# Cross attention on one core: the denominators' last sum moves from a transfer to TensorE, with another order of work in a step

## The chip, the cores and the metric

The kernel runs on one core of a Trainium2 chip. The metric is the device time of one execution in microseconds (us). The kernel before takes 3871.87 us (median of 3 runs, 3871.11 to 3872.05).

The engines are named as in the profile: PE is TensorE (PEld are its weight loads), DVE is VectorE, ACT is ScalarE, POOL is GpSimd, and SP issues transfers only.

## The reference, cut to what matters

```
q = (x @ Wq + bq)      # 4 batches x 1024 rows, 32 heads of 32
k = ctx @ Wk + bk      # 4 batches x 1601 rows,  8 key heads of 32
v = ctx @ Wv + bv
scores = einsum('bkgld,bksd->bkgls', q, k) / sqrt(32) + mask
attn   = softmax(scores, axis=-1)                 # over the 1601 keys
out    = einsum('bkgls,bksd->bkgld', attn, v) @ Wo + bo + x
result = layernorm(out) * gamma + beta
```

Each key head serves four query heads. All data is float32. The softmax's denominators, one sum over 1601 keys for each head and query row, are what the change is about.

## The kernel before, in words

There are three stages: `project` (q, k and v, stored to DRAM), `attend` (from about 0.8 to 3.48 ms of the span), and `output` (the last projection and the layer norm). Only `attend` is touched.

`attend` makes 64 steps: 8 blocks of 512 query rows times 8 key heads. A step takes 512 rows and the 4 query heads of one key head. Its 1601 keys are cut into 13 tiles of 128 (the last has 65). A step's work on TensorE is of five kinds, and the string `ORDER` writes it out as letters, 99 of them, in the order in which TensorE runs them:

- L (52 in a step: 13 tiles x 4 heads): one logit tile, keys x rows, into one of 3 PSUM banks `logit` (L866). ScalarE takes the exponential of it into the SBUF buffer `weights` (L1030). An L waits until the bank's previous user is read: the L three before it.
- S (32): half of a row of scores for the **next** step, two matmuls into one of 2 PSUM tiles `score` (L821). VectorE reduces it to a maximum (L972). An S waits for the reduction of the S two before it.
- M (13): one weights tile times its values, accumulated in `mixed` (L876, through `sum_heads`: four heads side by side, each on 32 columns of the array, in two passes: 8 matmul records). With `FIRST_MIX = 1` the first M of a step handles the last tile of the step before.
- T (1): the row maxima are transposed (L852); ScalarE and VectorE copy them (L1036, L984) and SP carries them to the next step's operands.
- P (1): the denominators of the step before, a matmul with ones (`denominators`, through `sum_heads`, L876); ScalarE copies them out (L1048). P shares the 3 `logit` banks with L and T.

The order is fixed by hand in `ORDER`; all engines but GpSimd loop over the same string. Each engine takes its instructions strictly in that order.

GpSimd sums the weights tiles of a step for the denominators. Tiles 0, 1, 3, 4, 6, 7, 9, 10 and 12 (the tuple `POOL`) are added by eight tensor_tensor instructions into `sum_pool` (`add`, L736). The other four, `REST = (2, 5, 8, 11)`, are summed by three accumulating transfers that GpSimd issues: tiles 5, 8 and 11 are added onto tile 2's own buffer, the base buffer (`add_rest`, L747). A fourth transfer, `merge` (L754), adds the base buffer to `sum_pool`; it is issued behind the first add of the next step, and waits for all eight adds and all three transfers. P waits for that transfer (`rest_merged`). The weights buffers are rings: 2 base buffers, 4 for the tiles of `POOL`, 2 for tiles 5, 8 and 11; ScalarE waits before it writes a buffer until the tile that was there is mixed and summed (in `exponents`). For the base buffer that wait is on `rest_merged`. The last step of all has its own end, `last_denominators`.

Of the kernel before, what the change touches and what calls it, by code (L numbers as in the profile page):

```python
# [22 lines left out]
ALU = mybir.AluOpType  # L23
ACT = mybir.ActivationFunctionType

P = 128
# [436 lines left out]
def attend(nc, mask_flat, q_dram, k_dram, v_dram, a_dram, d_dram, r_dram, wo_dram, ident, mask_size, qk_store, wo_spare, wo_in):  # L463
    QUAD = 4
# [3 lines left out]
    REST = (2, 5, 8, 11)  # L468
# [3 lines left out]
    LATE = 10  # L472
    NPOOL = len(POOL) - 1

    ORDER = "LLLSLSLLSLMSLLSLMMSLLSLLSLSLLSLMMSLLSLLSLSLLSLMMSLLSLLSLSLLSLPMMLSLSLLLSLSTMMLLSLLSLSLLSLSLLSLMMSLS"
    FIRST_MIX = 1
    LO_AT = 24
    assert [ORDER.count(k) for k in "LSMTP"] == [ST * G, 2 * NROW, ST, 1, 1]
    BANKS = 3
    USES = [k for k in ORDER if k in "LTP"]  # L480
    assert len(USES) % BANKS == 0
    TURN, SUMS = USES.index("T"), USES.index("P")
# [20 lines left out]
    def ring(st):  # L503

        return (POOL, RINGS[0], BASES) if st in POOL else (REST[1:], RINGS[1], BASES + RINGS[0])

    def buffer(s, st):

        if st == REST[0]:
            return s % BASES  # L510
        tiles, size, first = ring(st)
        return first + (s * len(tiles) + tiles.index(st)) % size
# [9 lines left out]
    with ExitStack() as held:  # L522
# [3 lines left out]
        def sem(name):  # L526
            return held.enter_context(nc.semaphore(name))
# [11 lines left out]
        weights = [sb(f"weights{i}", [P, G, LQ]) for i in range(BASES + sum(RINGS))]  # L539
        sum_pool = [sb(f"sum_pool{i}", [P, G, LQ]) for i in range(2)]  # L540
        ones = sb("ones", [P, HD])
# [6 lines left out]
        logit = [held.enter_context(nc.psum_tensor(f"logit{i}", [P, LQ], F32)) for i in range(BANKS)]  # L548
# [23 lines left out]
        pool_added = sem("pool_added")  # L572
        pool_seen = sem("pool_seen")
        rest_added = sem("rest_added")
        rest_merged = sem("rest_merged")
        mix_done = sem("mix_done")
        mixed_copied = sem("mixed_copied")
        denom_done = sem("denom_done")
# [138 lines left out]
        @block.gpsimd  # L717
        def _(pool):

            nc.gpsimd.memset(ones[:], 1.0).then_inc(const_done, 1)  # L720
            for i, k in enumerate(k_sb):
                pool.wait_ge(const_done, 1 + i)
                nc.gpsimd.memset(k[STACK:SHIFT, :].bitcast(F32), 1.0).then_inc(const_done, 1)

            def add(quad, s, n):

                step, st = quad * QUAD + s, POOL[n + 1]
                w = min(P, S - st * P)
                pool.wait_ge(exp_done, quad * (QUAD * ST * G) + (s * ST + st + 1) * G)
                if n == 0:  # L730
                    pool.wait_ge(denom_done, step + 1)
                    first = weights[buffer(s, POOL[0])]
                else:
                    pool.wait_ge(pool_added, step * NPOOL + n)
                    first = sum_pool[s % 2]
                nc.gpsimd.tensor_tensor(sum_pool[s % 2][0:w], first[0:w], weights[buffer(s, st)][0:w], ALU.add).then_inc(pool_added, 1)  # L736

            def add_rest(quad, s, k):

                step, st = quad * QUAD + s, REST[k]  # L740
                pool.wait_ge(exp_done, quad * (QUAD * ST * G) + (s * ST + st + 1) * G)
                if k == 1:
                    pool.wait_ge(mix_done, quad * (QUAD * ST) + (s * ST + REST[0] + 1 + MIX0))
                else:
                    pool.wait_ge(rest_added, step * (16 * (len(REST) - 1)) + 16 * (k - 1))
                pool.sem_inc(pool_seen, 1)
                pool.dma_start(weights[buffer(s, REST[0])][:], weights[buffer(s, st)][:], accum_op=ALU.add).then_inc(rest_added, 16)  # L747

            def merge(step, s):

                pool.wait_ge(pool_added, step * NPOOL + NPOOL)
                pool.wait_ge(rest_added, step * (16 * (len(REST) - 1)) + 16 * (len(REST) - 1))
                pool.sem_inc(pool_seen, 1)
                pool.dma_start(sum_pool[s % 2][:], weights[buffer(s % QUAD, REST[0])][:], accum_op=ALU.add).then_inc(rest_merged, 16)  # L754

            def sums(quad, s, first=False, last=False):
                for n in range(NPOOL):
                    if last and POOL[n + 1] >= LATE:
                        break
                    for k, st in enumerate(REST):  # L760
                        if k and POOL[n] < st < POOL[n + 1]:
                            add_rest(quad, s, k)
                    add(quad, s, n)
                    if n == 0 and not first:
                        merge(quad * QUAD + (s - 1), s - 1)

            pool.wait_ge(flag_done, 1)
            any_mask = pool.value_load(flag[0:1, 0:1], min_val=0, max_val=1)

            def clamp_max(a, lts):  # L770
                for lt in lts:
                    pool.wait_ge(mask_in[lt], a * 16 + 16)

                    pool.sem_inc(mask_max_seen, 1)
                    nc.gpsimd.tensor_scalar(mask_max[:, lt, :], mask_max[:, lt, :], -FAR, None, ALU.max).then_inc(mask_ready[lt], KVH // QUAD)

            def clamp_exp(a):
                pool.wait_ge(mask_exp_in, a * (16 * NLT) + 16 * NLT)

                pool.sem_inc(mask_exp_seen, 1)  # L780

                nc.gpsimd.tensor_scalar(mask_exp[:], mask_exp[:], -FAR, None, ALU.max).then_inc(mask_exp_ready, KVH // QUAD)

            def queries(a, first=False, final=False):
                with pool.If(any_mask > 0):
                    clamp_exp(a)
                for n in range(KVH):
                    if n >= KVH - 2 and not final:
                        with pool.If(any_mask > 0):
                            clamp_max(a + 1, range(0, 2) if n == KVH - 2 else range(2, NLT))  # L790
                    sums(a * (KVH // QUAD) + n // QUAD, n % QUAD, first and n == 0, final and n == KVH - 1)

            with pool.If(any_mask > 0):
                clamp_max(0, range(NLT))
            queries(0, first=True)
            for a in range(1, NLQ - 1):
                queries(a)
            queries(NLQ - 1, final=True)

        @block.tensor  # L800
        def _(pe):
# [71 lines left out]
            def sum_heads(out, lhs, rhs, w, start, stop):  # L873

                for h in range(G):
                    last = nc.tensor.matmul(out[h * HD:(h + 1) * HD, :], lhs, rhs[0:w, h, :], start=start, stop=stop)  # L876
                return last
# [11 lines left out]

            def denominators(step, s):  # L890

                pe.wait_ge(rest_merged, step * 16 + 16)
                sum_heads(logit[SUMS % BANKS], ones[:], sum_pool[s % 2], P, True, True).then_inc(denom_done, 1)

            def last_denominators():

# [10 lines left out]
            def quad_steps(quad, masked, first=False, last=False):  # L907
                for s in range(QUAD):
                    u = k = 0
                    tile = s * ST - FIRST_MIX  # L910
                    for work in ORDER:
                        if work == "L":
# [96 lines left out]
        def _(act):  # L1009
# [3 lines left out]
            def exponents(quad, s, u):  # L1013
                n = USES[:u].count("L")
                st, h = n // G, n % G
                before, old = tile_before(s, st)
                if h == 0 and not (isinstance(quad, int) and quad == 0 and before < 0):

                    if st == REST[0]:
                        act.wait_ge(rest_merged, quad * (16 * QUAD) + (16 * before + 16))  # L1020
                    else:
                        act.wait_ge(mix_done, quad * (QUAD * ST) + (before * ST + old + 1 + MIX0))

                        if old in POOL:
                            act.wait_ge(pool_added, quad * (QUAD * NPOOL) + (before * NPOOL + max(POOL.index(old), 1)))
                        else:
                            act.wait_ge(rest_added, quad * (QUAD * 16 * (len(REST) - 1)) + 16 * (before * (len(REST) - 1) + REST.index(old)))
                act.wait_ge(logit_done, quad * (QUAD * ST * G) + ((s * ST + st) * G + h + 1 + LOGITS0))
                w = min(P, S - st * P)
                nc.scalar.activation(weights[buffer(s, st)][0:w, h, :], logit[u % BANKS][0:w, :], ACT.Exp).then_inc(exp_done, 1)  # L1030
# [19 lines left out]
            def quad_steps(quad, first=False, last=False):  # L1050
                for s in range(QUAD):
                    u = mixes = 0
                    for work in ORDER:
                        if work == "L":
# [259 lines left out]
```

## Time and profile before

| | us |
|---|---|
| time, median of 3 runs | 3871.87 |
| the profiled execution's own time | 3873.77 |
| its span | 3872.1 |
| PE busy in the span | 3769.2 |
| DVE busy | 2496.9 |
| ACT busy | 2033.2 |
| POOL busy | 2895.5 |

The page gives the busy time of each engine, its groups of instructions by line, and the issues of transfers. "Busy" of PE includes the modelled end of each matmul, so a PE that is busy all the time is not at its peak. The timeline merges instructions of one kind that follow one another: a row has its start, the time that it covers, and behind x the number of instructions. In the timeline the weight loads (PEld) show best when TensorE begins a piece of work. POOL's L747 and L754 rows are issues of transfers; the transfers themselves run on the DMA queues.

### The profile page before, as it was taken

The numbers are of one execution on the slowest core, as the hardware profiler recorded it, in microseconds if no ns is written. First come the engines' busy times: TensorE is split into PE (matmuls) and PEld (weight loads), VectorE is DVE, ScalarE is ACT, GpSimd is POOL, SyncE is SP. The second block draws the span as 40 slices with busy tenths as digits, with TensorE's granted clock in tenths as the row PEclk, the third lists the DMA queues.
The fourth block names the chain that finished last, engine by engine and source line by source line (L and its number), as shares of the span: only waits on it lengthen the run. The fifth ranks groups of instructions, "written<-read, shape, count | busy, mean of one in ns | idle before, by whom it ended". The sixth has DMA issues, their size and how long they took to land. (4 is left out here: it accounts for less than half of the span.)

```text
span 3872.1 us, 55400 instructions
## 1 busy us (share of the span) xinstructions
PE 3769.2 (97%) x20306; PEld 2379.7 (61%) x20306; DVE 2496.9 (64%) x2904; ACT 2033.2 (53%) x3854; POOL 2895.5 (75%) x1104
## 2 busy tenths in 40 slices
PE   8999999789999999999999999999999999988998
PEld 7998888545555555555555555555555555536886
DVE  3334444477777777777777777777777777725665
ACT  2222112126666666666666666676666666661110
POOL 1111111139999999999999999999999999984555
PEclk9999999869999999999999999999999999998999
DMA  5344555647667667667667667677677677667664
GB/s 176 136 150 177 201 198 200 246 85 152 146 146 155 145 145 158 143 145 159 146 144 158 145 146 158 141 151 155 139 155 151 141 155 149 146 150 220 194 191 125
DMA packets 294100, 611.94 MB, mean 158 GB/s; under 512 B 131696, under 2 KB 168688, under 8 KB 261360
## 3 DMA queue, kind: packets, MB, share of 16 engines
q0 software_dynamic: 58080, 337.15, 38.7%
q1 hardware_dynamic: 232528, 265.54, 25.7%
q10 hardware_dynamic: 3264, 6.29, 0.5%
q8 instruction: 134, 2.20, 0.2%
q14 instruction: 94, 0.77, 0.1%
HBM read 244.50 MB, written 96.99 MB: 88 GB/s over the span
## 5 line engine op out<-in xcount | busy, mean ns | idle before, releaser
L972 DVE TENSOR_REDUCE half_max<-score 128x1 f32<-128x800 f32 (+1 forms) x2048 | 1893.7, 986 | 714.2 <-PE score L821 710.2
L1030 ACT ACTIVATE weights<-logit 128x512 f32<-128x512 f32 (+1 forms) x3328 | 1732.4, 602 | 791.6 <-PE logit L866 765.6
L736 POOL TENSOR_TENSOR sum_pool<-sum_pool,weights 128x2048 f32<-128x2048 f32 x446 | 2125.6, 4766 | 29.6 <-ACT weights L1030 2.5
L821 PE MATMUL score<-qk_store 96*128 96x400 f32 (+1 forms) x4096 | 1212.2, 378 | 14.9 <-DMA qk_store<-k_parts 10.4
L866 PE MATMUL logit<-qk_store 98*128 98x512 f32 (+1 forms) x3328 | 1199.5, 417 | 2.3 <-ACT weights L1030 2.2
L821 PEld LDWEIGHTS score<-qk_store 96*128 96x128 f32 x4096 | 688.5, 191 | 552.6 <-DVE half_max L972 397.5
L876 PE MATMUL mixed<-weights,v_sb 128*32 128x512 f32 x6656 | 807.8, 599 | 0.7 <-ACT weights L1030 0.7
L866 PEld LDWEIGHTS logit<-qk_store 98*128 98x128 f32 (+1 forms) x3328 | 607.8, 185 | 264.0 <-ACT weights L1030 135.1
L876 PEld LDWEIGHTS mixed<-weights,v_sb 128*32 128x32 f32 x6656 | 177.0, 109 | 393.2 <-ACT weights L1030 218.6
L736 POOL TENSOR_TENSOR sum_pool<-weights 128x2048 f32<-128x2048 f32 x64 | 313.7, 4901 | 63.6 <-ACT weights L1030 63.6
L450 POOL DMA_DIRECT2D q_parts<-o_hi x64 | 34.5, 540 | 306.1 <-DVE o_lo L412 149.3
L1192 PE MATMUL acc<-qk_store,a_hi 128*128 128x512 f32 x576 | 187.0, 397 | 25.1 <-DVE a_lo L1227 25.1
L347 ACT ACTIVATE o_hi<-summed,bq_scaled 128x512 fp32r<-128x512 f32 x64 | 44.1, 689 | 304.0 <-PE summed L259 274.3
L325 ACT CAST t_hi<-turned 128x512 fp32r<-128x512 f32 x168 | 95.6, 585 | 141.8 <-PE turned L254 141.8
L407 DVE TENSOR_SCALAR full<-summed,bq_scaled 128x512 f32<-128x512 f32 x64 | 48.0, 751 | 188.5 <-ACT o_hi L347 188.5
L747 POOL DMA_DIRECT2D weights<-weights x191 | 165.9, 868 | 0.0
L1281 POOL TENSOR_TENSOR total<-total,beta_row 128x1024 f32<-128x1024 f32 x32 | 100.4, 3139 | 76.3 <-DVE total L1248 76.3
L1274 POOL TENSOR_TENSOR total<-total,bo_row 128x1024 f32<-128x1024 f32 x32 | 89.6, 2806 | 85.4 <-DMA total<-in_x 85.2
L456 POOL DMA_DIRECT2D v_rows<-v_store x52 | 28.1, 540 | 160.1 <-DMA v_rows<-v_store 101.5
L1192 PEld LDWEIGHTS acc<-qk_store,a_hi 128*128 128x128 f32 x576 | 109.4, 190 | 52.6 <-issue 26.0
L372 DVE TENSOR_TENSOR t_lo<-turned,t_hi 128x512 fp32r<-128x512 f32 x168 | 113.1, 685 | 42.6 <-ACT t_hi L325 42.4
L259 PE MATMUL summed<-t_hi,wq_hi 128*128 128x512 f32 x512 | 134.6, 404 | 0.0
(87 smaller groups left out, 2772.4 us busy)
## 6 DMA issues: line engine op xcount, KB each, us to landing
weights<-weights POOLq DMA_DIRECT2D x191, 1024.0 KB, 7.3
sum_pool<-weights POOLq DMA_DIRECT2D x63, 1024.0 KB, 7.0
qk_store<-q_parts SPq DMA_DIRECT2D x192, 256.0 KB, 3.9
qk_store<-k_parts SPq DMA_DIRECT2D x192, 200.1 KB, 5.4
rows<-in_ctx SPq DMA_DIRECT2D x26, 1024.0 KB, 5.1
landing<-in_mask_Bx1xSxS_ff SPq DMA_DIRECT2D x32, 800.5 KB, 5.5
rows<-in_x SPq DMA_DIRECT2D x16, 1024.0 KB, 5.1
q_parts<-o_hi POOLq DMA_DIRECT2D x64, 256.0 KB, 2.4
```

The source lines that it names most:

```text
L259: last = nc.tensor.matmul(acc, lhs, rhs, start=(n == 0), stop=(n == len(pairs) - 1))
L325: nc.scalar.copy(t_hi[par][:, t, :], turned[t % 2][:]).then_inc(hi_done, 1)
L372: nc.vector.tensor_tensor(t_lo[par][:, t, :], turned[t % 2][:], t_hi[par][:, t, :].bitcast(F32), ALU.subtract).then_inc(lo_done, 1)
L736: nc.gpsimd.tensor_tensor(sum_pool[s % 2][0:w], first[0:w], weights[buffer(s, st)][0:w], ALU.add).then_inc(pool_added, 1)
L747: pool.dma_start(weights[buffer(s, REST[0])][:], weights[buffer(s, st)][:], accum_op=ALU.add).then_inc(rest_added, 16)
L821: last = nc.tensor.matmul(score[j][:, c, 0:w], q_sb[buf][0:STACK, h, lt * P:(lt + 1) * P], k_sb[buf][0:STACK, start:start + w], start=True ...
L866: last = nc.tensor.matmul(bank[0:w, :], k_sb[s][:, keys], q_sb[s][:, h, :], start=True, stop=not masked, skip_group_check=masked)
L876: last = nc.tensor.matmul(out[h * HD:(h + 1) * HD, :], lhs, rhs[0:w, h, :], start=start, stop=stop)
L972: nc.vector.tensor_reduce(half_max[m // NROW % 2][:, k % G, k // G, j:j + 1], score[j][:, :, 0:HALVES[j][2]], mybir.AxisListType.XY, ALU.m ...
L1030: nc.scalar.activation(weights[buffer(s, st)][0:w, h, :], logit[u % BANKS][0:w, :], ACT.Exp).then_inc(exp_done, 1)
L1192: last = nc.tensor.matmul(acc[j * NT + t][:, n, :], a[:, k, cols], w[k][:, out_cols], start=(k == 0 and m == 0), stop=(k == KVH - 1 and m ...
L1281: nc.gpsimd.tensor_tensor(total[r][:], total[r][:], beta_row[:], ALU.add).then_inc(final, 1)
```

## The change

`merge`, its call and its semaphore go. `denominators` takes two sums into one bank: first the base buffer, as soon as the step's three transfers are in, then `sum_pool`, when the eight adds are done. ScalarE's wait for the base buffer is now on the denominators of two steps back. `ORDER` is another string of the same letters.

```
-    ORDER = "LLLSLSLLSLMSLLSLMMSLLSLLSLSLLSLMMSLLSLLSLSLLSLMMSLLSLLSLSLLSLPMMLSLSLLLSLSTMMLLSLLSLSLLSLSLLSLMMSLS"
+    ORDER = "LLSSMSLLSLLSLLSLLSLSLLSLLSLLSLLSLLSLLSMMMMPSLLSLLSLLSLSLLSLLSLLSMMMSLLSLTSMMSLSLLLSLSLLSLLSLLSLMMML"
@@ GpSimd
-            def merge(step, s):
-                pool.wait_ge(pool_added, step * NPOOL + NPOOL)
-                pool.wait_ge(rest_added, step * (16 * (len(REST) - 1)) + 16 * (len(REST) - 1))
-                pool.sem_inc(pool_seen, 1)
-                pool.dma_start(sum_pool[s % 2][:], weights[buffer(s % QUAD, REST[0])][:], accum_op=ALU.add).then_inc(rest_merged, 16)
...
-                    if n == 0 and not first:
-                        merge(quad * QUAD + (s - 1), s - 1)
@@ TensorE, denominators
-                pe.wait_ge(rest_merged, step * 16 + 16)
-                sum_heads(logit[SUMS % BANKS], ones[:], sum_pool[s % 2], P, True, True).then_inc(denom_done, 1)
+                pe.wait_ge(rest_added, step * (16 * (len(REST) - 1)) + 16 * (len(REST) - 1))
+                sum_heads(logit[SUMS % BANKS], ones[:], weights[buffer(s % QUAD, REST[0])], P, True, False)
+                pe.wait_ge(pool_added, step * NPOOL + NPOOL)
+                sum_heads(logit[SUMS % BANKS], ones[:], sum_pool[s % 2], P, False, True).then_inc(denom_done, 1)
@@ ScalarE, exponents
                     if st == REST[0]:
-                        act.wait_ge(rest_merged, quad * (16 * QUAD) + (16 * before + 16))
+                        act.wait_ge(denom_done, quad * QUAD + (before + 3))
```

## Rows read from the trace of the kernel before

**Rows 1.** The page, busy us and share of each engine.
```profile
PE 3769.2 (97%) x20306; PEld 2379.7 (61%) x20306; DVE 2496.9 (64%) x2904; ACT 2033.2 (53%) x3854; POOL 2895.5 (75%) x1104
```
**Rows 2.** The windows view, full steps 0 to 62: busy us, granted clock, DMA share.
```profile
841.10:3441.00 2599.90, 2596.91 (x14408) 1425.95 (x14407) 1876.05 (x2142) 1788.87 (x3470) 2525.37 (x755) 1.00 0.70 148
```
**Rows 3.** The waits view, 1000 to 3400 us: us in total, times, longest.
```profile
ACT weights L1030 <- PE logit L866: 689.0, 465, 2.3
DVE half_max L972 <- PE score L821: 649.1, 409, 2.5
PEld score L821 <- DVE half_max L972: 345.9, 878, 0.8
...
POOL sum_pool L754 <- DMA weights<-weights: 31.8, 29, 2.1
...
POOL sum_pool L736 <- ACT weights L1030: 0.9, 2, 0.4
```
**Rows 4.** Groups of POOL by form, 1000 to 3400 us: count, busy, mean ns, idle before.
```profile
L736 POOL TENSOR_TENSOR sum_pool<-sum_pool,weights 128x2048 f32<-128x2048 f32 x349 | 1656.6, 4747 | 25.7 <-ACT weights L1030 0.9
...
L747 POOL DMA_DIRECT2D weights<-weights x175 | 151.9, 868 | 0.0
L754 POOL DMA_DIRECT2D sum_pool<-weights x58 | 52.3, 902 | 42.1 <-DMA weights<-weights 31.8 <-POOL sum_pool L736 6.8 <-issue 3.3
```
**Rows 5.** Timeline of ACT: the copy behind each step's first M.
```profile
2034.67 0.59 ACT L1042 COPY mixed_sb<-mixed 128x512 f32<-128x512 f32 x1 [0.26 <-PE mixed L876]
...
2075.92 0.59 ACT L1042 COPY mixed_sb<-mixed 128x512 f32<-128x512 f32 x1 [0.25 <-PE mixed L876]
...
2117.19 0.59 ACT L1042 COPY mixed_sb<-mixed 128x512 f32<-128x512 f32 x1 [0.26 <-PE mixed L876]
```
**Rows 6.** Timeline of POOL: first adds of two steps, the merge between.
```profile
2038.16 4.91 POOL L736 TENSOR_TENSOR sum_pool<-weights 128x2048 f32<-128x2048 f32 x1
2043.33 0.87 POOL L754 DMA_DIRECT2D sum_pool<-weights  x1 [0.26 <-POOL sum_pool L736]
2043.93 9.64 POOL L736 TENSOR_TENSOR sum_pool<-sum_pool,weights 128x2048 f32<-128x2048 f32 x2
...
2079.00 4.91 POOL L736 TENSOR_TENSOR sum_pool<-weights 128x2048 f32<-128x2048 f32 x1
```
**Rows 7.** Timeline of weight loads, within one step and the next one's start.
```profile
2006.49 0.30 PEld L821 LDWEIGHTS score<-qk_store 96*128 96x128 f32 x2 [0.23 <-DVE half_max L972]
2006.78 0.19 PEld L866 LDWEIGHTS logit<-qk_store 98*128 98x128 f32 x1
2007.29 0.16 PEld L876 LDWEIGHTS mixed<-weights,v_sb 128*32 128x32 f32 x8 [0.32 <-ACT weights L1030]
...
2009.15 0.30 PEld L821 LDWEIGHTS score<-qk_store 96*128 96x128 f32 x2 [0.84 <-DVE half_max L972]
...
2013.48 0.16 PEld L876 LDWEIGHTS logit<-sum_pool,ones 128*32 128x32 f32 x8 [0.32 <-ACT weights L1030]
...
2016.19 0.19 PEld L866 LDWEIGHTS logit<-qk_store 98*128 98x128 f32 x1 [0.84 <-issue]
...
2021.56 0.30 PEld L866 LDWEIGHTS logit<-qk_store 98*128 98x128 f32 x2 [0.84 <-issue]
...
2033.54 0.16 PEld L876 LDWEIGHTS mixed<-weights,v_sb 65*32 65x32 f32 x8 [0.31 <-ACT weights L1030]
2034.53 0.30 PEld L821 LDWEIGHTS score<-qk_store 96*128 96x128 f32 x2 [0.84 <-DVE half_max L972]
```
**Rows 8.** Timeline of DVE: the reductions of two stretches.
```profile
2009.83 4.59 DVE L972 TENSOR_REDUCE half_max<-score 128x1 f32<-128x804 f32 x5 [1.59 <-PE score L821]
...
2022.69 5.64 DVE L972 TENSOR_REDUCE half_max<-score 128x1 f32<-128x800 f32 x6 [1.73 <-PE score L821]
```
**Rows 9.** Timeline of ACT: the exponentials of one stretch.
```profile
2010.06 4.20 ACT L1030 ACTIVATE weights<-logit 128x512 f32<-128x512 f32 x8 [1.97 <-PE logit L866]
```
**Rows 10.** The page, issues of transfers: KB each, median us to landing.
```profile
weights<-weights POOLq DMA_DIRECT2D x191, 1024.0 KB, 7.3
```

More of the change, by code:

```diff
@@ L574, in attend @@
         rest_added = sem("rest_added")
-        rest_merged = sem("rest_merged")
         mix_done = sem("mix_done")
```

## The prediction, before the run

> **What bounds the kernel now.** The page comes first: TensorE is busy for 97% of the span, GpSimd for 75% [rows 1]. Both are candidates, so the stage that the change touches is read alone: from 841.1 to 3441.0 us, 63 steps at 41.27 us each, TensorE shows 2597 of 2600 us busy and GpSimd 2525 of 2600, at the full clock (1.00, 2.4 GHz) [rows 2]. Busy time can't decide between them; the waits do. ScalarE and VectorE wait for TensorE (689 and 649 us in 2400), TensorE waits for VectorE's reductions (346 us), and there is no row of any weight in which somebody waits for GpSimd's adds; GpSimd waits for ScalarE 2 times in all, for 0.9 us, and for its own transfers 31.8 us, all at the merge [rows 3]. The beat tells the rest: the copy behind the first M comes at 2034.67, 2075.92 and 2117.19, steps of 41.25 and 41.27 [rows 5], while one GpSimd step is 40.84 [rows 6]. So the loop of TensorE, ScalarE and VectorE sets the step, and GpSimd is close under it with about 0.4 us of room.
>
> Inside a step TensorE alternates between groups of M (with P) and stretches of L and S. A group of two M lasts from 2007.29 to 2009.15, 1.86 us; one M 0.99 (2033.54 to 2034.53); P with two M 2.71 (2013.48 to 2016.19) [rows 7]. Each M or P more is 0.86, and 0.13 to 0.14 is fixed. In a group ScalarE and VectorE run dry: 1.97 and 1.59 us idle behind two M [rows 8, 9]. In the stretch of 5 S and 8 L between (2009.15 to 2013.48, 4.33 us) VectorE starts 0.68 behind TensorE and reduces without a gap, 5 in 4.59; the last one covers 0.99, so the pitch is 0.90. ScalarE does 8 exponentials in 4.20, a pitch of at most 0.51, with a gap where an S held TensorE; I take 0.49 for a run without gaps (an estimate from the same row). VectorE is what such a stretch waits for: 32 x 0.90 = 28.8 us a step against 52 x 0.49 = 25.5.
>
> **The merge goes.** GpSimd loses an issue that costs it 0.60 of its step (2043.33 to 2043.93) [rows 6] and a wait of 42.1/58 = 0.73 [rows 4]. Its adds and three other issues remain, 40.84 - 0.60 - 0.26 - 0.4 (an estimate: the add behind the merge starts without the overlap that adds have) = 39.6 us. TensorE's step stays above that, so the gain is 0 us on the path; the cover is TensorE's loop, and if GpSimd had been the bound it would be worth up to 1.3 us a step. 63 transfers of 1 MB leave the queues; no waits for loads stand in the loop, so again nothing.
>
> **P doubles.** A second sum_heads of the same shape as an M, on the path, since TensorE takes everything in order: 0.86 us a step, 63 times = 54 us, if it stood in the old order. Bounds: 0.86 by P with two M against two M; at least 0.86 - 0.14 = 0.72 if it fell into a drain.
>
> **The new waits.** P now waits for the transfers and then for the adds itself; behind it in TensorE's queue stands all of the work. Before, the last add of a step ends where the next first add starts, 2038.16, 4.6 us behind the first M of the new step (2033.54), and the third transfer lands about 8 us behind its issue, which comes before that last add: about 8 us behind that M [rows 6, 7, 10]. In the new order P stands after 21 L, 12 S and 4 M more: over 14 us behind the first M. So cost 0; the cover is 6 us, and if GpSimd ran later by more than that, each us would be paid in full. ScalarE's wait for the base buffer is on the P of two steps back, done a step earlier: 0. The M of tiles 0 to 3 come late (after 23 L instead of 10 to 18), so ScalarE may find ring buffers occupied: tile 6 needs the M of tile 0, which stands right before its L; tile 4 needs the add of tile 12, done about 3 us before: 0. GpSimd will wait instead, for tile 9's exponentials (L 37 to 40 come only behind three groups), about 2 us a step, in its own spare time.
>
> **The new order.** Counting letters, five groups instead of seven: M; MMMMP; MMM; MM; MMM. With the double P these are 1, 6, 3, 2 and 3 units: 0.99 + 5.29 + 2.71 + 1.86 + 2.71 = 13.56 us, against 0.99 + 5 x 1.86 + 2.71 = 13.0 before. What counts is the stretches, 41.26 - 13.0 = 28.3 us before. I walk them with these rules [rows 7 to 9]: the first reduction starts 0.68 behind a leading S (1.13 behind LLS: 2021.56, 2022.69), further ones follow at 0.90; an S starts 0.05 behind the end of the reduction two before; a group starts 0.80 behind the last S where one L stands between (2006.49 to 2007.29), and I take 0.63 where the S is last (bounds 0.51, which is L to M, and 0.80).
> - L of the old step's end, LLSS, M, then 12 S and 21 L up to MMMMP. Both PSUM sets are empty, so LLL and SS start at once and the first M begins 1.6 behind; it is covered for VectorE, which has two reductions (first at 1.32) to do. 14 reductions by VectorE alone: last one starts at 1.32 + 13 x 0.90 = 13.0, the group 0.13 earlier: 12.9. But most of it is LLS, LLS: ScalarE needs 2 x 0.49 = 0.98 for what VectorE does in 0.90, and starts only at 3.5, behind the copy of mixed. Its 18th exponential ends at 3.5 + 17 x 0.49 + 0.6 = 12.4, the last L then the last S and the group follow at 0.05, 0.11 and 0.63 more: 13.2. I take 13.25, with the M in it.
> - SLLSLLSLLSLSLLSLLSLLS (8 S, 13 L): last S at 0.68 + 5 x 0.90 + 0.99 + 0.05 = 6.2, group at 6.85; with short slips of the LLS pattern 6.95.
> - SLLSLTS: T needs the first exponential (1.5), the last S then 1.75, group 2.4.
> - SLSLLLSLSLLSLLSLLSL (7 S, 12 L): 0.68 + 6 x 0.90 + 0.04 = 6.12 by VectorE, 6.25 by ScalarE; 6.2.
>
> Sum: 13.25 + 5.29 + 6.95 + 2.71 + 2.4 + 1.86 + 6.2 + 2.71 = 41.37. The stretch of 6 S in the old order lasted 0.16 more than the pitch says (6 reductions in 5.64, not 5.49) [rows 8], and the new order has more runs with both engines at their limit, so I add 0.05: **41.42 a step, 0.16 more than before**. 62 steps carry the S: +10 us. The last two lose their S, keep the longer groups: +1 (bounds -1 and +3). The profiled execution took 3873.77, its span 3872.1, 1.67 less; 3873.77 + 11 = 3884.8. The median shown is 1.90 under that execution: **3883 us**. A change of 0.2%, 7.7 us, is about what a measurement of this kernel can tell from none.
>
> **A rule against the row.** The first M behind an L loads its weights 0.51 us behind the L (2006.78 to 2007.29), where a load itself takes 0.19, and 0.13 is lost on the way out [rows 7]. 0.32 + 0.14 twice a step is 0.92, just over what P costs: if every group paid this on the path, the new order's two groups less would leave the step where it was. The Trainium skill, TensorEngine Tiling (Array Packing), Key Properties, says that changing the array's tiling mode drains TensorE; by that rule, fewer groups are worth their drains. My walk credits them only where no engine behind has work left.
>
> **Rivals.**
> - *No change*, by the drains just worked out: 41.25 + 0.86 - 0.92 = 41.19, times 62 is -4: 3868; with the walk's small errors 3864 to 3879. For it: the two terms are both read from rows. Against: in the old order VectorE's 0.95 us of work left covered part of each drain.
> - *Faster: the LLS runs keep VectorE's pitch.* If the 3 banks hide ScalarE's 0.98 and no tie is lost, the stretches are 12.9, 6.85, 2.3 and 6.12 and the step is 13.56 - 0.99 + 28.2 = 40.75, -0.5 x 62 = -31: 3841. Place: the long stretch behind the first M; it decides for faster from a sum of stretches 0.3 us under mine. For it: VectorE had no gap in any stretch of five. Against: no stretch of the old order has more than two LLS in a row.
> - *The order gives nothing back*: +0.86 a step, 3926. For it: one group of six units leaves ScalarE and VectorE dry for 5 us at once. Against: a gap's length has no price of its own, only the sum of units.
> - *GpSimd was the bound*: its step of 41.27 falls by 1.33, at 62 steps -82: 3790. Against: the waits and the steady 41.25.
>
> **Chances.** Slower by little, as forecast (3880 to 3898): 0.34; slower with more lost ties (to 3915): 0.12; order gives nothing: 0.05. No change: 0.24. Faster by kept pitch (3841 to 3864): 0.22; GpSimd: 0.03. Slower 0.51, same 0.24, faster 0.25. The range leaves out the order-gives-nothing case, GpSimd and the far part of the faster one: 3847 to 3912; the likeliest case's own is 3876 to 3898.
>
> **What would show it.** The copy behind the first M comes every 41.4 us; the group MMMMP lasts 5.3 us; VectorE waits in the long stretch by a few hundredths each LLS; GpSimd idles about 1.8 us a step, for ScalarE; no wait of TensorE for transfers or adds before P. A beat under 41.1 or over 41.8, or a wait before P, proves the walk wrong; a stretch over 13.6 or under 13.0 says where.

## The result, and the profile after

The changed kernel takes 3885.86 us (median of 6 executions, 3883.19 to 3890.43) against 3871.96 for the kernel before in the same runs: a ratio of 1.0037, 95% interval 1.0024 to 1.0050. It is slower by 14 us, 0.36%; the forecast was 3883 and slower. The profiled execution took 3883.19, with a span of 3881.5: 9.4 more than before. One of a12's four executions ran far longer than the rest (8956 us) and is left out of its ratio; the median of 3829.08 given there counts it, and is 3828.74 without it.

The page's first line, as [rows 1]: GpSimd is busy for less, TensorE for more.

```profile
PE 3778.4 (97%) x20810; PEld 2405.8 (62%) x20810; DVE 2508.6 (65%) x2904; ACT 1990.5 (51%) x3854; POOL 2835.8 (73%) x1041
```

The waits of the changed kernel, 1000 to 3400 us (us in total, times, longest), as [rows 3]:

```profile
DVE half_max L964 <- PE score L811: 637.7, 232, 4.9
ACT weights L1022 <- PE logit L856: 471.2, 291, 3.1
ACT denom_sb L1040 <- PE logit L866: 278.7, 58, 4.8
...
PEld logit L856 <- ACT weights L1022: 192.2, 786, 0.4
PEld score L811 <- DVE half_max L964: 182.3, 432, 0.8
...
POOL sum_pool L735 <- ACT weights L1022: 96.1, 73, 1.7
```

and one of GpSimd's waits in its timeline, before tile 9:

```profile
2107.73 9.31 POOL L735 TENSOR_TENSOR sum_pool<-sum_pool,weights 128x2048 f32<-128x2048 f32 x2 [1.73 <-ACT weights L1022]
```

The reader is to see two things. ScalarE and VectorE still wait for TensorE, as before, but in fewer and longer waits (up to 4.9 us, during MMMMP). And GpSimd now waits for ScalarE, 73 times, where it had waited for it twice; its waits for transfers are gone with the merge.

One step of the changed kernel in the timeline of weight loads, as [rows 7]; each row's start is where TensorE begins that piece:

```profile
2106.13 0.30 PEld L811 LDWEIGHTS score<-qk_store 96*128 96x128 f32 x2 [0.84 <-DVE half_max L964]
...
2112.33 0.16 PEld L866 LDWEIGHTS mixed<-weights,v_sb 128*32 128x32 f32 x8 [0.35 <-ACT weights L1022]
...
2115.04 0.48 PEld L856 LDWEIGHTS logit<-qk_store 98*65 98x65 f32 x3 [0.84 <-issue]
...
2116.61 0.16 PEld L866 LDWEIGHTS mixed<-weights,v_sb 65*32 65x32 f32 x8 [0.26 <-ACT weights L1022]
2117.61 0.30 PEld L811 LDWEIGHTS score<-qk_store 96*128 96x128 f32 x2 [0.84 <-DVE half_max L964]
...
2127.67 0.42 PEld L811 LDWEIGHTS score<-qk_store 96*128 96x128 f32 x2
2128.36 0.16 PEld L866 LDWEIGHTS mixed<-weights,v_sb 128*32 128x32 f32 x8 [0.27 <-issue]
...
2131.83 0.13 PEld L866 LDWEIGHTS logit<-weights,ones 128*32 128x32 f32 x4 [0.30 <-issue]
2132.26 0.13 PEld L866 LDWEIGHTS logit<-sum_pool,ones 128*32 128x32 f32 x4 [0.30 <-issue]
...
2133.65 0.30 PEld L811 LDWEIGHTS score<-qk_store 96*128 96x128 f32 x2 [0.84 <-issue]
...
2140.57 0.16 PEld L866 LDWEIGHTS mixed<-weights,v_sb 128*32 128x32 f32 x8 [0.27 <-issue]
...
2143.29 0.30 PEld L811 LDWEIGHTS score<-qk_store 96*128 96x128 f32 x2 [0.84 <-issue]
...
2145.58 0.16 PEld L866 LDWEIGHTS mixed<-weights,v_sb 128*32 128x32 f32 x8 [0.27 <-ACT weights L1022]
...
2147.43 0.30 PEld L811 LDWEIGHTS score<-qk_store 96*128 96x128 f32 x2 [0.84 <-DVE half_max L964]
```

Differences of the starts give the walk's terms as measured:

| piece | walked | measured |
|---|---|---|
| LLL SS, M, 12 S and 21 L (2115.04 to 2128.36) | 13.25 | 13.32 |
| MMMMP, six units (to 2133.65) | 5.29 | 5.29 |
| 8 S, 13 L (to 2140.57) | 6.95 | 6.92 |
| MMM (to 2143.29) | 2.71 | 2.72 |
| SLLSLTS (to 2145.58) | 2.4 | 2.29 |
| MM (to the next start, 2147.43) | 1.86 | 1.85 |
| 7 S, 12 L (2106.13 to 2112.33) | 6.2 | 6.20 |
| MMM (to 2115.04) | 2.71 | 2.71 |

The sum is 41.3. The rows of VectorE for the long stretch and the next, as [rows 8], show 14 reductions in 13.12 us where the pitch alone gives 0.99 + 13 x 0.90 = 12.7, and the dry time behind them:

```profile
2116.36 13.12 DVE L964 TENSOR_REDUCE half_max<-score 128x1 f32<-128x800 f32 x14 [3.15 <-PE score L811]
2134.32 5.57 DVE L964 TENSOR_REDUCE half_max<-score 128x1 f32<-128x800 f32 x6 [4.85 <-PE score L811]
```

The step's beat in the timeline of ScalarE, the copy behind the first M, as [rows 5]: 41.34 and then 41.56. In 61 full steps the mean was 41.24 before and is 41.40 now.

```profile
2034.84 0.59 ACT L1034 COPY mixed_sb<-mixed 128x512 f32<-128x512 f32 x1 [0.66 <-PE mixed L866]
...
2076.18 0.59 ACT L1034 COPY mixed_sb<-mixed 128x512 f32<-128x512 f32 x1 [0.66 <-PE mixed L866]
...
2117.74 0.59 ACT L1034 COPY mixed_sb<-mixed 128x512 f32<-128x512 f32 x1 [0.65 <-PE mixed L866]
```

The account: 61 x 0.152 = 9.3 us, all but 0.1 of the profile's difference. The first copy comes 4 us earlier than before, and from the end of these steps to the end of the span it is 4 us more. The two belong together, since the first M now stands behind 4 letters of a step and not behind 10. The granted clock is 1.00 in all of these 61 steps in both kernels.

### The profile page after: what moved, and what is told of

Read it like the earlier page. It is cut to its first block and busy times, and to the rows that moved or that the text cites. A ratio compares the mean times of both kernels' runs of the same rounds, so it can differ in the third digit from the quotient of the medians.

```text
span 3881.5 us, 56282 instructions
## 1 busy us (share of the span) xinstructions
PE 3778.4 (97%) x20810; PEld 2405.8 (62%) x20810; DVE 2508.6 (65%) x2904; ACT 1990.5 (51%) x3854; POOL 2835.8 (73%) x1041
## 5 line engine op out<-in xcount | busy, mean ns | idle before, releaser
L735 POOL TENSOR_TENSOR sum_pool<-sum_pool,weights 128x2048 f32<-128x2048 f32 x446 | 2071.6, 4645 | 139.9 <-ACT weights L1022 102.7
L1022 ACT ACTIVATE weights<-logit 128x512 f32<-128x512 f32 (+1 forms) x3328 | 1689.1, 615 | 540.1 <-PE logit L856 532.5
L811 PE MATMUL score<-qk_store 96*128 96x400 f32 (+1 forms) x4096 | 1177.4, 372 | 15.9 <-DMA qk_store<-k_parts 10.6
L856 PE MATMUL logit<-qk_store 98*128 98x512 f32 (+1 forms) x3328 | 1179.7, 423 | 1.2 <-ACT weights L1022 0.8
L811 PEld LDWEIGHTS score<-qk_store 96*128 96x128 f32 x4096 | 705.4, 191 | 405.6 <-DVE half_max L964 220.2
L866 PE MATMUL mixed<-weights,v_sb 128*32 128x512 f32 x6656 | 783.3, 599 | 0.9 <-ACT weights L1022 0.9
L1040 ACT COPY denom_sb<-logit 128x512 f32<-128x512 f32 x64 | 37.6, 587 | 307.5 <-PE logit L866 307.5
```

The costliest lines, as they stand in the source:

```text
L811: last = nc.tensor.matmul(score[j][:, c, 0:w], q_sb[buf][0:STACK, h, lt * P:(lt + 1) * P], k_sb[buf][0:STACK, start:start + w], start=True ...
L856: last = nc.tensor.matmul(bank[0:w, :], k_sb[s][:, keys], q_sb[s][:, h, :], start=True, stop=not masked, skip_group_check=masked)
```

## The experiments

The theory: TensorE's fixed order, with ScalarE and VectorE behind it, sets the step in both kernels; the second sum costs what an M costs; the new order gives most of it back. The main rival: GpSimd, close under the bound, has a part in it.

**a1, the new order alone.** Only the string `ORDER` of the kernel before is replaced.

> The new order of work alone; the merging transfer and the single sum of the denominators stay. Theory (TensorE's loop sets the step, the second sum costs 0.86 us a step): without the second sum the loop would need 41.39 - 0.86 = 40.53 us a step. GpSimd with its merge needs 40.45 at the least in the kernel before and 40.84 in a usual step, plus its wait for transfers, so it becomes the bound: steps of 40.6 to 41.1 us, 3837 to 3866 us in all, and ScalarE or TensorE begin to wait for GpSimd. Rival (the new order by itself is slower, the second sum is hidden): 3880 or more. Rival (GpSimd's merge is free, nothing else binds): 3832.

Measured: 4231.39 us, ratio 1.0951 (1.0932 to 1.0971). All three expectations were wrong. The time lies in the first rival's "3880 or more", but not for its reason: a2 shows that the second sum is not hidden. The waits of a1, 1000 to 3400 us:

```profile
PE logit L876 <- DMA sum_pool<-weights: 203.2, 51, 4.9
POOL sum_pool L736 <- ACT weights L1030: 169.8, 103, 2.7
```

The new order has P after 23 L, and there the merging transfer has not landed; in GpSimd's timeline the merge is issued at 2012.07, and in TensorE's P starts at 2019.15:

```profile
2005.17 4.95 POOL L736 TENSOR_TENSOR sum_pool<-weights 128x2048 f32<-128x2048 f32 x1
2012.07 0.87 POOL L754 DMA_DIRECT2D sum_pool<-weights  x1 [1.95 <-DMA weights<-weights]
```
```profile
2019.15 1.94 PE L876 MATMUL logit<-sum_pool,ones 128*32 128x512 f32 x8 [4.07 <-DMA sum_pool<-weights]
```

TensorE stands, so ScalarE's exponentials and with them GpSimd's adds come later, so the next merge does too: each engine waits for the other once a step, and steps last 44 to 49 us. With P in that place the new order could not have been had while the merge stayed.

The wait is not all of it. While TensorE stands, its granted clock falls from 1.00 to 0.50, which is 1.2 instead of 2.4 GHz, and P and the work behind it run at that level. P takes 1.94 us above (1.06 in a7 at full clock, shown below), and two L take 1.06 where they take 0.62. The windows view of the wait and of the stretch behind it (as [rows 2]), then the two rows of L:

```profile
2012.00:2016.00 4.00, 3.08 (x32) 0.67 (x24) 0.54 (x1) 0.06 (x1) 3.93 (x2) 1.00 0.66 135
2020.00:2024.00 4.00, 4.00 (x16) 2.70 (x9) 1.38 (x2) 1.69 (x3) 2.44 (x2) 0.50 0.01 2
```
```profile
2005.64 0.62 PE L866 MATMUL logit<-qk_store 98*128 98x512 f32 x2
...
2021.85 1.06 PE L866 MATMUL logit<-qk_store 98*128 98x512 f32 x2
```

Of the first 61 steps of a1, 7 have the full clock throughout and last 44.14 us on average. The other 54 have such a stretch and last 47.20. The mean is 46.85, against 40.54 in a2, which has the same order: about 3.6 us of the difference stand in the steps with the full clock, and about 2.7 go with the clock.

**a2, one sum.** The changed kernel, the base buffer's sum left out of P.

```
                 pe.wait_ge(rest_added, ...)
-                sum_heads(..., ones[:], weights[buffer(s % QUAD, REST[0])], P, True, False)
                 pe.wait_ge(pool_added, ...)
-                sum_heads(..., ones[:], sum_pool[s % 2], P, False, True)
+                sum_heads(..., ones[:], sum_pool[s % 2], P, True, True)
```

> The changed kernel with the sum of the base buffer left out of the denominators (tiles 2, 5, 8 and 11 are missing from them); both waits stay. It prices the second sum in its place and frees GpSimd of the merge. Theory: a step of 41.39 - 0.86 = 40.53 us, 63 steps, 3886 - 54 = 3832 us. Rival (the second sum lies in the shade of ScalarE's and VectorE's work): 3880 to 3886.

Measured: 3833.69, ratio 0.9903 (0.9888 to 0.9918), steps of 40.49 and every fourth of 40.71, 40.54 on average. The second sum is on the path: 41.40 less 40.54 is 0.85 us a step. The order is worth 36.6 us against the 3870.24 of the kernel before, or 0.70 a step (41.24 less 40.54), if the merge that is also missing here is worth nothing, which a6 shows in the old order.

**a3, the parts in the old order.** `ORDER` of the changed kernel is the old one, with P moved from ahead of the fifth group to ahead of the third (`...SLLSLPMMSLLS...`), where it stands before tile 5's weights.

> The old order of work with the merging transfer dropped and the second sum in; P alone is moved, from ahead of the M of tile 6 to ahead of the M of tile 2, so that it stands before tile 5's weights. Theory: the second sum is paid in full, 0.86 x 63 = 54 us over the kernel before: 3926 us (3918 to 3930), steps of 42.1. Rival (the merge was worth something, GpSimd's wait was on the path): 3880 to 3905. Rival (the second sum falls into the drain of the group): 3872 + 45 = 3917 or less.

Measured: 3973.85, ratio 1.0260 (1.0246 to 1.0274): 104 us over the kernel before, twice the theory's 54. Its waits name one reason:

```profile
PE logit L866 <- DMA weights<-weights: 31.4, 35, 1.8
```

P stands after 18 L, where the third transfer has often not landed, in 35 of some 56 steps. These 31 us are not all: in the same 2400 us, a3 lost 44 more than the second sum (mean step 42.90, and 42.11 in a5 below). The rest has no row of its own. **a5** tests that by putting P back in its old place. For that, the transfers of even and odd steps count on two semaphores, so that the wait of P stays unambiguous when tile 5 of the next step is already under way.

```
-        rest_added = sem("rest_added")
+        rest_added = [sem(f"rest_added{i}") for i in range(2)]      # every use takes [s % 2]
```

> The old order, P in its old place, the merging transfer dropped and the second sum in. The three transfers of even and odd steps count on two semaphores, so that P may stand behind tile 5. Theory (a3 lost about 50 us because P stood before the transfers had landed, and 54 us for the second sum): here P comes some 12 us later, nothing waits, and the second sum alone is paid: 3870 + 54 = 3924 us, steps of 42.1. Rival (the second sum costs more than an M in the old order, or GpSimd without its merge disturbs others): 3945 to 3975 as in a3.

Measured: 3924.91, ratio 1.0138 (1.0121 to 1.0155), steps of 42.11, and no wait for a transfer. **a6** is a5 with the base buffer's sum left out, as a2.

> As a5, with the sum of the base buffer left out of the denominators (tiles 2, 5, 8 and 11 missing from them); the old order, no merging transfer, one sum. Theory (the merge was hidden in the kernel before): same as before, 3870 us, steps of 41.25, while GpSimd gains over 1 us a step and waits for ScalarE instead. Rival (GpSimd was the bound, or the merge's 63 MB slowed somebody): 3790 to 3860.

Measured: 3870.96, ratio 0.9997 (0.9987 to 1.0006). a5 less a6 is 53.95 us, 0.856 for each of 63 steps: the price of the second sum. a6 against the kernel before: the merge cost nothing there, though GpSimd now waits for ScalarE (88.5 us in 2400).

**a4, the fourth step.** The changed kernel's `if s == 2 and k == 8` becomes `k == 14`: the reciprocal moves into the group MMMMP.

> The changed kernel with VectorE's reciprocal of the denominators (15 times, 0.54 us) moved from behind the 8th reduction of the step to behind the 14th, where VectorE runs dry during the group MMMMP. Every fourth step of the changed kernel is 41.56 instead of 41.34 long. Theory (in the long stretch VectorE is as much at its limit as ScalarE, so 0.54 us on it can't be hidden): all steps 41.34, 15 x 0.22 = 3.3 us less, 3882.5. Rival (the longer fourth step has another cause, the transfers of that step): no change, 3886.

Measured: 3885.1, ratio 1.0037 (1.0024 to 1.0051). In the profile the longer fourth step is gone: the step that was 41.56 is 41.31 (2077.23 to 2118.54), with the reciprocal in the dry time. The rows are VectorE's, then ScalarE's copies:

```profile
2075.84 13.12 DVE L964 TENSOR_REDUCE half_max<-score 128x1 f32<-128x800 f32 x14 [3.16 <-PE score L811]
2088.88 0.54 DVE L972 RECIPROCAL dens<-dens 128x64 f32<-128x64 f32 x1
```
```profile
2077.23 0.58 ACT L1034 COPY mixed_sb<-mixed 128x512 f32<-128x512 f32 x1 [0.66 <-PE mixed L866]
...
2118.54 0.58 ACT L1034 COPY mixed_sb<-mixed 128x512 f32<-128x512 f32 x1 [0.66 <-PE mixed L866]
```

The profiled execution is 2.0 us shorter (3881.22 against 3883.19). The median does not show the 3 us: executions of this kernel spread over 8 us. The mechanism is shown by the steps, the gain in the time is not.

**a7, the second sum on VectorE.** One addition behind the 14th reduction replaces it.

```
+                dve.wait_ge(rest_added, ...); dve.wait_ge(pool_added, ...)
+                nc.vector.tensor_tensor(sum_pool[s % 2][:], sum_pool[s % 2][:], weights[buffer(s % QUAD, REST[0])][:], ALU.add).then_inc(sums_merged, 1)
```

> The changed kernel with the second sum of TensorE replaced by one VectorE addition of the base buffer to sum_pool, behind the 14th reduction of the step, where VectorE runs dry for 4.9 us during MMMM. Theory: an addition of 128x2048 takes 2.3 us (as a_in's does), it is done before TensorE has finished the four M, TensorE's step loses 0.86 us: 40.5 a step, 3834 us, under both kernels. GpSimd may be held up by VectorE during the addition; it has 1.7 us a step to spare. Rival (the addition ends after the four M): the step loses less, each us late is paid, 3850 to 3890. Rival (GpSimd is held up by more than its spare time): over 3860 with ScalarE waiting for GpSimd's adds.

Measured: 4020.41, ratio 1.0378 (1.0360 to 1.0395), outside all three expectations. Three timelines of a7: VectorE's addition, GpSimd's two adds beside it, and TensorE's P.

```profile
2023.96 4.54 DVE L972 TENSOR_TENSOR sum_pool<-sum_pool,weights 128x2048 f32<-128x2048 f32 x1
```
```profile
2021.77 11.20 POOL L736 TENSOR_TENSOR sum_pool<-sum_pool,weights 128x2048 f32<-128x2048 f32 x2
```
```profile
2028.65 1.06 PE L867 MATMUL logit<-sum_pool,ones 128*32 128x512 f32 x8 [2.07 <-DVE sum_pool L972]
```

The addition takes 4.54 us where its length alone (`a_in` in the output stage) is 2.28, and GpSimd's pair 11.2 where it is 9.3 in the changed kernel. P waits for it, as in the first rival, 108.6 us in 2400 or 1.97 a step. ScalarE has no row of waiting for GpSimd's adds, so it is not the second rival. With the full clock a step lasts 42.72, 2.2 more than a2's. But here too the clock falls behind many of the waits:

```profile
2071.00:2075.00 4.00, 3.62 (x13) 1.85 (x14) 0.92 (x2) 0.85 (x2) 4.00 (x1) 0.57 0.02 4
```

Of the first 61 steps, 29 keep the full clock. The other 32 last 44.37 on average, so that the mean is 43.59: another 0.87 a step, 53 us in all. **a8** adds the reciprocal's move (`k == 14`).

> As a7, with VectorE's reciprocal (15 times, 0.54 us) moved behind that addition, into the same gap. Theory: every fourth step loses its extra 0.2 us, 15 x 0.21 = 3 us under a7, 3831. Rival: the gap is full, no difference or slower.

Measured: 4033.59, ratio 1.0417 (1.0399 to 1.0434). The time is the rival's, but the gap is not full: in the step of the profile that has the reciprocal (2162.64), VectorE still waits 2.24 us for the next S behind it. A step with the full clock lasts 42.74, as in a7. What differs is how many have it: 21 of 61, where a7 has 29. Eight more steps that are 1.6 us longer are 13 us, the whole difference. Why the clock falls more often in a8 is not shown.

**a9, the merge kept, P later.** The kernel before in the new order, with P ahead of the next group: `...SMMMMSLLS...LLSPMMMSLLSL...`.

> The kernel before (merging transfer, one sum) in the new order, with one letter moved: P stands ahead of the next group, PMMM, after 36 L instead of 23. Theory (a1 lost 6 us a step because P came before the merging transfer had landed, which it does some 20 us into the step; the order itself is the faster one): P comes at 26 us, nothing waits, TensorE's step is 40.5; GpSimd with its merge needs 40.5 to 40.9, so 40.5 to 41.0 a step: 3835 to 3858 us, under both kernels. Rival (the merge's waits hold GpSimd up further in the new order, whatever P does): steps over 42, over 3920.

Measured: 3896.87, ratio 1.0066 (1.0054 to 1.0078). P no longer waits, but the time lies between those of the theory and the rival. The steps begin at 40.5:

```profile
916.27 0.59 ACT L1042 COPY mixed_sb<-mixed 128x512 f32<-128x512 f32 x1 [0.66 <-PE mixed L876]
956.78 0.59 ACT L1042 COPY mixed_sb<-mixed 128x512 f32<-128x512 f32 x1 [0.67 <-PE mixed L876]
997.27 0.58 ACT L1042 COPY mixed_sb<-mixed 128x512 f32<-128x512 f32 x1 [0.66 <-PE mixed L876]
```

and then GpSimd, which needs longer, has fallen behind, and ScalarE waits for its adds; the mean step is 41.55. The waits, 1000 to 3400 us:

```profile
POOL sum_pool L754 <- DMA weights<-weights: 55.0, 46, 1.9
...
ACT weights L1030 <- POOL sum_pool L736: 38.9, 40, 1.8
```

Here GpSimd is the bound. The clock has a share in this too: in 9 of the first 61 steps it falls, and they last 43.8. The other 52 have a mean of 41.17, still 0.6 over the loop of TensorE. **a10** has P one group later still (`TSPMM`).

> As a9, with P one group later still, ahead of the MM behind T (30 us into the step). Theory (nothing waits for P's transfer in a9 already): the same time as a9 within 5 us. Rival (GpSimd late at P in a9): 10 us or more under a9.

Measured: 3900.93, ratio 1.0072 (1.0059 to 1.0084), as a9. **a11** is a9 with the reciprocal at `k == 14`.

> As a9, with VectorE's reciprocal moved behind the 14th reduction, into the group MMMM. Theory: every fourth step loses its extra 0.2 us where TensorE's loop is the bound, up to 3 us under a9. Rival (GpSimd bounds a9): no difference.

Measured: 3898.51, ratio 1.0070 (1.0058 to 1.0083): no difference, the rival. **a12** takes away GpSimd's wait, from a10, with the reciprocal at `k == 14`:

```
-                    if n == 0 and not first:
+                    if n == 1 and not first:
                         merge(quad * QUAD + (s - 1), s - 1)
```

> As a10 (merging transfer, one sum, new order, P ahead of the MM behind T), with the merge issued behind the second add of the next step instead of the first, and VectorE's reciprocal in the group MMMM. In a9 and a10 GpSimd lost about 1 us a step waiting for the third transfer before the merge, and ScalarE then waited for GpSimd's adds. Theory (GpSimd's wait at the merge is what holds a9 at 41.4 a step): 4.6 us later the third transfer has landed, GpSimd needs about 40.2 a step, TensorE's loop of 40.5 is the bound again: 3832 to 3845 us, under both kernels. Rival (GpSimd is slowed by something else, or P now waits for the later merge): 3860 or more, with rows of TensorE waiting for the merging transfer.

Measured: **3829.08 us**, ratio 0.9890 (0.9870 to 0.9909), 42 us under the kernel before, below both, and 3 us under the theory's range. GpSimd's merge has no idle time before it any more, and the beat is 40.51 and 40.46. By a10 and a11, neither the later P nor the moved reciprocal does anything while GpSimd is the bound, so it is the later merge that lifts the bound. First its group (count, busy, mean ns, idle before), then the waits and the copies:

```profile
L754 POOL DMA_DIRECT2D sum_pool<-weights x60 | 52.1, 869 | 0.0
```
```profile
ACT weights L1030 <- POOL sum_pool L736: 3.5, 2, 3.1
```
```profile
2008.42 0.59 ACT L1042 COPY mixed_sb<-mixed 128x512 f32<-128x512 f32 x1 [0.65 <-PE mixed L876]
2048.93 0.59 ACT L1042 COPY mixed_sb<-mixed 128x512 f32<-128x512 f32 x1 [0.66 <-PE mixed L876]
2089.39 0.59 ACT L1042 COPY mixed_sb<-mixed 128x512 f32<-128x512 f32 x1 [0.65 <-PE mixed L876]
```

## Why the prediction was right

- **The bound.** TensorE's loop sets the step before and after. Shown by a6: without the merge GpSimd has spare time and nothing becomes faster. But GpSimd's room was about 0.2 us and not 0.4. In a6 it waits 88.5 us in 58 steps, 1.5 a step, and the merge had taken 1.33 of that; the prediction's 40.84 was one GpSimd step and not their mean. With the loop at 40.5, GpSimd with its merge (a9) sets steps of 41.17 at full clock and a mean of 41.55.
- **The second sum**: 0.86 predicted, 0.856 in the old order (a5 less a6). In the new order the mean steps of the changed kernel and of a2 differ by 0.85.
- **The merge gone**: 0 predicted, and a6 is 1.5 us under the kernel before, inside the noise. What the prediction missed is what it is worth beside the new order. P in its early place would wait for the merge (a1), and even with P late the merge's wait makes GpSimd the bound (a9). The merge's removal is what lets the order's 36.6 us be had; the second sum then takes more than that.
- **The new waits**: 0 at P, right, there is no row of TensorE waiting for transfers or adds. How close it was shows in a3, where P after 18 L cost 49 us over a5, in the old order; the changed kernel has it after 23. GpSimd's own wait for ScalarE before tile 9 was put at 2 us; the timeline shows 1.73, and all its waits for ScalarE are 96.1 us in 58 steps, 1.66 a step.
- **The order**: 41.42 a step predicted, 41.40 measured: 0.16 more than before, as forecast, since the order gives 0.70 of the 0.86. That it fits to 0.02 is luck, for two small errors cancel. Three steps of four last 41.34 and not 41.42: the long stretch took 0.07 more than walked, the one with T took 0.11 less, and the 0.05 that was added for lost ties did not show. The reciprocal of every fourth step, which the prediction did not have, costs 0.22 there (41.56, and 41.31 in a4), 15 times. That comes to 0.055 a step. In the old order it cost nothing: VectorE's dry time behind that stretch was 1.18 instead of 1.59 us and took it up.
- **The rivals.** *Faster, the LLS runs keep the pitch*: wrong, 14 reductions took 13.12 and not 12.7. *No change by drains*: the whole order gives 0.70 a step (a2), less than the 0.92 that this rival gave to two groups less. A group's entry behind an S takes 0.69 (2127.67 to 2128.36), near the 0.63 assumed. No run takes away two groups and leaves the stretches as they are, so what part of the 0.70 is drains stays open. *The order gives nothing*: wrong, a5 is what that would be. *GpSimd the bound*: wrong here, right in a9.
- **The ends**: +1 predicted, about 0.1 in the profile.
- What stays open: medians differ by 13.9 us, the two profiled executions by 9.4. The account above explains the 9.4, not the other 4.5. Further executions of the changed kernel took up to 3890.4, and none of the longer ones was profiled.

## What to carry to other kernels

Walk an in-order engine piece by piece, with starts from the timeline, and let each piece end where the slowest of its followers lets it; here that gave each of eight pieces within 0.11 us. When an order is changed, compare each fixed-rate helper with the new, shorter step and not with the old one: an engine with a few tenths of a microsecond to spare was hidden in one order and the bound in the other. Before a transfer is dropped and its work moved to a busier engine, try to issue it one instruction later: in a12, with P moved too, that removed the wait and gave the fastest kernel of all. When a change makes TensorE wait, read the granted clock beside the waits: in a1 and a7 the waits explain only part of the loss.

## What the runs showed that was not expected

VectorE's addition of two SBUF operands and GpSimd's adds exclude each other. In a7 VectorE's begins at 2023.96; GpSimd's first add of that pair, begun at 2021.77, should end some 4.6 us later, at 2026.3, and 2.28 us after that is 2028.6, when VectorE's is over (2028.5). GpSimd's pair is longer by 1.9. If the two only shared the speed of a port, VectorE's addition would take the same time wherever it begins. It does not: begun 2.19 us into GpSimd's add it takes 4.54, and begun 2.89 us into it, in another step, it takes 3.84. It ends 6.73 us behind the start of GpSimd's add both times.

```profile
1457.89 3.84 DVE L972 TENSOR_TENSOR sum_pool<-sum_pool,weights 128x2048 f32<-128x2048 f32 x1 [0.34 <-DMA weights<-weights]
```
```profile
1455.00 11.17 POOL L736 TENSOR_TENSOR sum_pool<-sum_pool,weights 128x2048 f32<-128x2048 f32 x2
```

The Trainium skill, SBUF — State Buffer, "SBUF: two separate sides", says that the two engines share a port pair as an exclusive lock held for a whole instruction, also for a VectorE operation with two SBUF inputs. These rows agree, within 0.2 us. VectorE's reductions, which read PSUM, show no such thing: their means are 983 and 988 ns in the kernel before, the changed one and a7.

A wait of TensorE can be paid beyond its own length: in a1 P waits 4.0 us a step (203.2 us, 51 times), and the mean step is 46.85 us where the order needs 40.54. The steps in which the clock stays at 1.00 last 44.14, less than the sum of the two. What is above that goes with the 1.2 GHz behind the wait, and not with the transfer.
